# A fused linear-attention and mixture-of-experts kernel on eight cores: another order of the experts, of the queue and of the small inputs

## The chip, the cores and the metric

The kernel runs on all eight cores of one Trainium2 chip. No core talks to another: core c takes one half of batch element c // 2, 1024 tokens that it writes, and reads the other half of that sequence as well, because the attention state sums over it. The metric is the device time of the slowest core in microseconds (us).

## The reference

Layer one is linear attention with 16 query heads over 4 key/value heads of width 128, on hidden states (4, 2048, 2048). In the kernel's staging each core works on the 2048 tokens of one sequence for K and V and on its own 1024 for everything else:

```
sq, sk = elu(q) + 1, elu(k) + 1
kv = sum over s of sk[s] v[s]^T ;  k_sum = sum over s of sk[s]
attn = (sq @ kv) / (sq . k_sum + 1e-6) ;  y = x + attn @ Wo.T ;  x2 = layernorm(y)
```

Layer two is a mixture of experts on x2, closed by a second layer norm:

```
h = x2 @ down_w ;  logits = x2 @ router_w - cost ;  top 2 of 8 experts, gates by softmax
out = sum over 2 picks of gate * (gelu(gelu(h) @ w1_e) @ w2_e + b2_e)      (w1_e: 1024 x HE[e])
out += 0.1 * (gelu(gelu(h) @ shared_w1) @ shared_w2)
y2 = x2 + out @ up_w + gelu(x2) @ core_w ;  result = layernorm(y2)
```

An expert that a token did not pick sees a zero row, and what it makes of a zero row is added too; the kernel takes that from one row of each expert's output (the "zero rows") by a small matmul with coefficients. HE is [1024, 2048, 3072, 4096] twice over, so experts 0 to 7 have 1, 2, 3, 4, 1, 2, 3, 4 groups of 1024 hidden units, 20 groups in all.

## The kernel before

**Weights.** All weights lie in HBM as float32. GpSimd's queue (called POOL in the profile) loads them in quarters of a block: one DMA of 128 x 2048 elements, 1 MB read and cast to 0.5 MB of bfloat16. Two quarters are a half. A group of an expert has four halves, two of w1 and two of w2.

**Stages.** (1) K and V of the four 512-token blocks, in the order 2, 3, 0, 1; block 2 is done quarter by quarter as its data lands, block 3 waits for all its four quarters. (2) Q, (3) the output projection Wo with residual and the sums for the layer norm, for token halves th = 0 and 1. (4) `router(0)` reads the float32 x2 of th 0; `down_tile(th, lc)` computes gelu(h) per 128 columns; `ln_stats` and `ln1_tile` normalize th 1 between them; then `router(1)`, `logits` and `routing`, which gives each token its two slots in the gather area `xg`. `grow_tile(ti)` transposes gelu(h) to token rows, and 16 scatters on POOL (8 tiles of 128 tokens, two picks) write them to `xg`. (5) The shared expert's first matrix, `shared1`, on TensorE. (6) The 20 groups: `xg_load` (on SyncE's queue, SP) and `xg_transpose` bring an expert's rows in; `gemm1` works on C = CAP[e] slots (448, 320, 256, 192, twice), `gemm2` on tiles of up to 128 of them; `y_store` writes `yd`. Between them lie `turn`, 8 calls that transpose x2 for the output, and `core_tile`, 32 tiles of gelu(x2) @ core_w, by the tables TURN and CORE. (7) The tail: `gather_low` and `gather_high` fetch each token's two rows of `yd`; the second shared matrix, the zero rows (`Rr`) and the gathered rows are summed in PSUM (`combine` scales and adds the gathered rows); then 8 tiles of 4 x 8 matmuls with up_w, the layer norm and the stores.

**Order of the weights.** `stream` is the list of halves in order of use: 80 for the experts, 2 for shared_w2 (SW2), 4 for up_w (UP0, UP1). `stream_into(slot, token)` puts the next half into a slot that comes free. Ten halves are placed ahead: C1 twice, B1 twice, D, B0 twice, E twice, S. `used` refills a slot after its last matmul, except the B slots, which become the store of gelu(x2), and D, which then holds core_w. So five half slots (C1, C1, E, E, S) carry the stream through the experts. POOL's queue is served in order: an instruction that waits holds all behind it. The scatters stand behind the two loads into B0, which wait for `t_d1`, the last down tile. `gather_low` stands in the stream, at group 17; `zero_row(e)`, a 2 KB load each, after each expert.

**Small inputs.** Ten small tensors and the matrix `sel` are loaded on SP at the start, 1.2 MB, unordered against the weights and x.

Of the kernel before, what the change touches and what calls it, by code (L numbers as in the profile page):

```python
# [29 lines left out]
BASE = np.cumsum([0] + CAP).tolist()  # L30
MAIN = BASE[NE]
# [3 lines left out]
GROUPS = [(e, g) for e in range(NE) for g in range(HE[e] // 1024)]  # L35
# [77 lines left out]
def build_nc():  # L113
# [9 lines left out]
    bq_t = din("bq_t", (128, 16))  # L123
    bk_b = din("bk_b", (128, 512))
    bv_b = din("bv_b", (128, 512))
    down_b_t = din("down_b_t", (128, 8))
    up_b_t = din("up_b_t", (128, 16))
    core_b_t = din("core_b_t", (128, 16))
    b1_t = din("b1_t", (128, NCH_TOT + 8))
# [44 lines left out]
    bqs = sb("bqs", (128, 16), F32)  # L174
    dbs = sb("dbs", (128, 8), F32)
    ubs = sb("ubs", (128, 16), F32)
    cbs = sb("cbs", (128, 16), F32)
# [1 line left out]
    b1s = sb("b1s", (128, NCH_TOT + 8), F32)
    rbb = sb("rbb", (128, 64), F32)  # L180
    cf = sb("cf", (128, 472), F32)
    ch = sb("ch", (128, 384), BF16)
# [1014 lines left out]
    xg_load(0)  # L1197
    xg_transpose(0)
    xg_load(1)
    for gi, (e, g) in enumerate(GROUPS):  # L1200
# [4 lines left out]
        if last and e + 1 < NE:
            xg_transpose(e + 1)
            if e + 2 < NE:
                xg_load(e + 2)
        for _ in range(CORE.get(gi, (0, 0))[0]):
            core_tile()  # L1210
        gemm2(gi)
        for th, q in TURN.get((gi, 2), []):
            turn(th, q)
        if last:
            y_store(e)
            if e:
                zero_row(e - 1)
        if e == NE - 2 and last:
            t_ylow = list(t_ydma)
# [8 lines left out]
    t_lastmm = u_free  # L1230
# [185 lines left out]

    for over, src in ((True, yd.ap()), (False, yd.ap()[0:MAIN, :])):
        kept = po.branch(None)
        if over:
            gather_low(src)  # L1420
        gather_high(src)
        po.join(kept, flg[0:1, 0:1], over)
# [86 lines left out]
def _stage_weights(inp):  # L1509
# [24 lines left out]
    m["bq_t"] = col(inp["L0_attn_bq"])  # L1534
    m["bk_b"] = f(np.broadcast_to(inp["L0_attn_bk"], (128, 512)))
    m["bv_b"] = f(np.broadcast_to(inp["L0_attn_bv"], (128, 512)))
    m["down_b_t"] = col(g("down_b"))
    m["up_b_t"] = col(g("up_b"))
    m["core_b_t"] = col(g("core_b"))
    m["b1_t"] = f(np.concatenate([col(g(f"e{e}_b1")) for e in range(NE)]  # L1540
                                 + [col(g("shared_b1"))], axis=1))
# [53 lines left out]
```

How the kernel before makes its waits and increments, by code:

```python
    def after(self, *toks):  # L63
        for tok in toks:
            if tok is None:
                continue
            c, val = tok
            if self.seen.get(id(c), 0) >= val:
                continue
            self.seen[id(c)] = val
            self.q.append(lambda eng, h=c.h, val=val: eng.wait_ge(h, val))
# [5 lines left out]
    def step(self, fn, *toks):  # L77
        self.after(*toks)
        c = self.count
        c.v += 1
        self.q.append(lambda eng, h=c.h: fn(eng).then_inc(h, 1))
        return (c, c.v)
# [1 line left out]
    def dma(self, c, out, in_, *toks):  # L84
        self.after(*toks)
        c.v += 16
        self.q.append(lambda eng, h=c.h: eng.dma_start(out, in_).then_inc(h, 16))
        return (c, c.v)
# [877 lines left out]
            def scat(e, ti=ti, k=k):  # L966
                return e.indirect_dma_start(
                    xg.ap(), bass.IndirectOffsetOnAxis(
                        ap=slt[:, k * 8 + ti:k * 8 + ti + 1], axis=0),
                    grow(ti), None).then_inc(c_sc.h, 16)
# [209 lines left out]
    def gather(c, dst, src, i):  # L1180
        return lambda e: e.indirect_dma_start(
            dst, None, src, bass.IndirectOffsetOnAxis(
                ap=slt[:, i:i + 1], axis=0)).then_inc(c.h, 16)
```

## Time and profile before

| | |
|---|---|
| median of 3 runs | 1264.79 us (1262.26 to 1277.39) |
| the profiled execution | 1255.26 us |
| its span, slowest core (core 7) | 1253.7 us |
| spans of the other cores | 1243.4 to 1250.7 us |
| TensorE matmul busy | 1061.4 us (85%) |
| VectorE, ScalarE, GpSimd busy | 432.9, 286.1, 219.2 us |
| POOL's DMA queue | 146.85 MB written, 73.2% of 16 engines' span |
| SP's DMA queue | 38.18 MB written, 9.9% |

The span runs from the first to the last instruction of a core; the time is 1.6 us more. All rows are of core 7. Columns DMA share and GB/s of a stretch say how busy the core's 16 DMA engines were and what they wrote; the share reads 1.07 in long stretches where the queue is never empty, so 1.07 and not 1 stands for full. A cast load counts its 0.5 MB written, not the 1 MB read.

### The profile page before, as it was taken

How to read it: one execution, taken by the hardware profiler on the slowest of the kernel's cores; microseconds unless marked ns; L12 is line 12 of the kernel's file. 1: busy time of each engine (PE TensorE's matmuls, PEld its weight loads, DVE VectorE, ACT ScalarE, POOL GpSimd, SP SyncE). 2: the span in 40 equal slices, each digit the busy share in tenths (PEclk: the TensorE clock that was granted, in tenths of full speed). 3: DMA queues.
4: the chain of work that ended last, by engine and by line, in shares of the span. 5: the costliest groups of instructions: out<-in, count | busy, mean ns of one | idle time of the engine just before them, and what ended most of it. 6: DMA issues, size and time to landing. Idle time of an engine off the chain costs nothing.

```text
span 1253.7 us, 18255 instructions; the slowest of 8 cores (1243.4 to 1253.7 us)
## 1 busy us (share of the span) xinstructions
PE 1061.4 (85%) x7106; PEld 591.7 (47%) x7106; DVE 432.9 (35%) x730; ACT 286.1 (23%) x489; POOL 219.2 (17%) x301
## 2 busy tenths in 40 slices
PE   4699999998999899789989678697987978735897
PEld 1244443433444344345657557563556757412443
DVE  0233334446679673026332111211211211100477
ACT  0100133442223344217221111111111111120234
POOL 7000100000010002401222222211222211511100
PEclk9899999999999999989999999998999988868899
DMA  9999591407269535985999999999999999999235
GB/s 158 168 166 164 83 211 56 68 1 137 65 124 189 100 57 78 235 167 122 192 165 173 180 168 166 180 176 199 165 187 171 162 185 170 204 192 198 94 101 168
DMA packets 95502, 186.29 MB, mean 149 GB/s; under 512 B 8055, under 2 KB 13303, under 8 KB 95408
## 3 DMA queue, kind: packets, MB, share of 16 engines
q0 software_dynamic: 73504, 146.85, 73.2%
q1 hardware_dynamic: 21904, 38.18, 9.9%
q8 instruction: 59, 0.97, 0.3%
q14 instruction: 35, 0.29, 0.1%
HBM read 291.73 MB, written 27.53 MB: 255 GB/s over the span
## 4 chain that ended last, share of the span: by engine, by line
PE 54%; DMA 30%; DVE 7%; issue 4%; POOL 2%; ACT 1%; DVEq 0%; SPq 0%; ACTq 0%; POOLq 0%
PE bk L248 53%; DMA rD<-wts 13%; DMA rC<-wts 7%; DVE ms L263 4%; DMA rE<-wts 3%; DMA rA<-x 3%; DMA smx<-yd 2%; DVE rA L263 2%; PE bk L252 2%; DMA ms<-xg 1%; POOL xg L967 1%; DMA yd<-ms 1%; ACT ms L260 1%; DMA xg<-ms,slt 1%; DVE ms L274 1%
## 5 line engine op out<-in xcount | busy, mean ns | idle before, releaser
L260 ACT ACTIVATE rC<-bk,b1s 128x192 bf16<-128x192 f32 (+3 forms) x160 | 76.7, 480 | 431.6 <-PE bk L248 427.8
L248 PE MATMUL bk<-rC 128*128 128x512 bf16 (+5 forms) x824 | 149.1, 337 | 27.8 <-DMA rC<-wts 26.5
L248 PE MATMUL bk<-rD,rB 128*128 128x128 bf16 x2048 | 126.2, 226 | 33.6 <-DMA rD<-wts 31.6
L248 PEld LDWEIGHTS bk<-rD,rB 128*128 128x128 bf16 x2048 | 122.7, 101 | 39.7 <-issue 38.7
L248 PEld LDWEIGHTS bk<-rC 128*128 128x128 bf16 (+1 forms) x824 | 79.0, 101 | 92.3 <-issue 48.4
L248 PE MATMUL bk<-rE,rC 128*128 128x512 bf16 (+1 forms) x416 | 99.0, 393 | 26.3 <-DMA rE<-wts 25.1
L263 DVE TENSOR_TENSOR rA<-rA,bk 128x512 f32<-128x512 f32 x64 | 43.3, 686 | 190.6 <-PE bk L248 190.6
L87 POOL DMA_DIRECT2D rC<-wts x72 | 51.5, 728 | 253.1 <-PE bk L248 227.8
L248 PE MATMUL bk<-rD,rA 128*128 128x512 bf16 x256 | 63.5, 405 | 29.6 <-DMA rA<-x 22.7
L87 POOL DMA_DIRECT2D rE<-wts x76 | 54.7, 729 | 172.3 <-PE bk L248 166.9
L248 PE MATMUL bk<-rC,rE 128*128 128x192 bf16 (+3 forms) x608 | 78.5, 288 | 1.6 <-DMA rE<-wts 1.6
L248 PEld LDWEIGHTS bk<-rE,rC 128*128 128x128 bf16 (+1 forms) x416 | 41.1, 103 | 80.0 <-issue 38.9
L263 DVE TENSOR_TENSOR ms<-ms,bk 128x512 f32<-128x512 f32 (+1 forms) x52 | 35.6, 685 | 112.1 <-PE bk L248 112.1
L277 DVE COPY ms<-bk 128x512 f32<-128x512 f32 (+2 forms) x50 | 34.5, 689 | 92.3 <-PE bk L248 85.9
L248 PEld LDWEIGHTS bk<-rC,rE 128*128 128x128 bf16 x608 | 55.8, 98 | 21.3 <-issue 2.3
L260 ACT ACTIVATE ms<-ms 128x512 f32<-128x512 f32 (+2 forms) x51 | 30.8, 606 | 123.1 <-DVE ms L267 87.8
L248 PE MATMUL bk<-rA 128*128 128x512 bf16 x256 | 57.9, 379 | 0.0
L248 PE MATMUL bk<-rE,rA 128*128 128x512 bf16 x256 | 57.9, 379 | 0.0
L87 POOL DMA_DIRECT2D rD<-wts x34 | 24.6, 727 | 180.4 <-PE bk L248 165.7
L248 PEld LDWEIGHTS bk<-rD,rA 128*128 128x128 bf16 x256 | 25.6, 103 | 62.3 <-issue 39.1
L248 PE MATMUL bk<-rC,rS 128*128 128x512 bf16 (+2 forms) x352 | 53.2, 309 | 0.0
L87 POOL DMA_DIRECT2D rS<-wts x38 | 27.3, 739 | 134.1 <-PE bk L248 125.1
(128 smaller groups left out, 1262.7 us busy)
## 6 DMA issues: line engine op xcount, KB each, us to landing
rE<-wts POOLq DMA_DIRECT2D x76, 512.0 KB, 27.2
rC<-wts POOLq DMA_DIRECT2D x72, 512.0 KB, 27.1
rS<-wts POOLq DMA_DIRECT2D x38, 512.0 KB, 28.0
rD<-wts POOLq DMA_DIRECT2D x34, 512.0 KB, 25.1
rA<-x POOLq DMA_DIRECT2D x16, 512.0 KB, 49.6
yd<-ms SPq DMA_DIRECT2D x16, 512.0 KB, 9.7
out<-rA SPq DMA_DIRECT2D x32, 256.0 KB, 2.9
rB<-wts POOLq DMA_DIRECT2D x12, 512.0 KB, 12.9
```

What stands on the lines that cost most here:

```text
L87: self.q.append(lambda eng, h=c.h: eng.dma_start(out, in_).then_inc(h, 16))
L248: return lambda e: e.matmul(o, lt, r, start=a, stop=z, skip_group_check=skip)
L252: return lambda e: e.transpose(o, i, idn)
L260: return lambda e: e.activation(o, i, f, **kw)
L263: return lambda e: e.tensor_tensor(o, a, b, op)
L274: return lambda e: e.reciprocal(o, i)
L277: return lambda e: e.tensor_copy(o, i)
L967: return e.indirect_dma_start(xg.ap(), bass.IndirectOffsetOnAxis(ap=slt[:, k * 8 + ti:k * 8 + ti + 1], axis=0), grow(ti), None).then_inc(c ...
```

## The change

1. **Experts.** The order is 3, 2, 1, 0, 4, 5, 6, 7: first 4 groups with C = 192, then 3 with 256, 2 with 320, 1 with 448; the last four experts stay. The slots of `xg` are laid out in that order. TURN and CORE are new tables, `xg_transpose` stands ahead of the turns.
2. **Down tiles.** Tiles 0, 1, 2 of th 0 are computed together, jc by jc (`down3`), each step as soon as its x2 is there; `ln_stats` of th 1 comes after 13 of 16 steps; `router(0)` moves behind down tile 7 and `logits(0)` behind `router(1)`. Router(1) uses bank 3.
3. **Scatters.** Each half of B0 is loaded after four tiles' scatters, not ahead of all 16. The load of b2 ahead of them is gone.
4. **End of the queue.** `gather_low` moves behind the last expert's and SW2's weights. The up weights leave the stream: UP0 is loaded behind the first four `gather_high`, UP1 behind the last four. The zero rows and b2 are loaded by SP after the last matmul of the experts, as float32, and copied to bfloat16 by VectorE.
5. **Small inputs.** Nine tensors become two: the K and V biases (0.5 MB), issued when the second quarter of block 2 has landed, and `sml_t` (0.49 MB), when block 0 has; `sel` follows. Banks of the first K and V tiles are renumbered, so that block 3 starts on banks that are evicted first.

```diff
+ORDER = [3, 2, 1, 0, 4, 5, 6, 7]
+BASE = [sum(CAP[f] for f in ORDER[:ORDER.index(e)]) for e in range(NE)]
-GROUPS = [(e, g) for e in range(NE) for g in range(HE[e] // 1024)]
+GROUPS = [(e, g) for e in ORDER for g in range(HE[e] // 1024)]
...
-        t_ld = sp.dma(c_ld, d_, s_.ap())
+    t_ld = sp.dma(c_ld, msl(0, 1024), bkv.ap(), xb[2][1])
+    t_sm = sp.dma(c_sm, sml[:], sml_t.ap(), xb[0][3])
...
+    KB = [2, 4, 0, 6]
-        kv_evict(s, s, 4 + s, tks[s], tvs[s])
+        kv_evict(s, KB[s], KB[s] + 1, tks[s], tvs[s])
...
+    ac.after(t_sm)
+    dv.after(t_sm)
+    pe.after(t_sm)
...
-    router(0)
-    down_tile(0, 0)
+    def down3(j0, j1):
+        for jc in range(j0, j1):
+            for lc in range(3):
+                pe.after(bfree[lc], dn[0][lc], t_x2b[0][jc])
+                f = mm(bank[lc][:], slot["C0"][:, lc * 2048 + jc * 128:
+                                               lc * 2048 + jc * 128 + 128],
+                       x2b(0, jc), jc == 0, jc == 15)
...
+    down3(0, 13)
     t_stat[1], t_mat = ln_stats(S1[1], S2[1], ys2[1], t_tmp[1])
-    down_tile(0, 1)
-    logits(0)
-    down_tile(0, 2)
+    down3(13, 16)
     for lc in range(3, 8):
         for oc in range(3 * lc - 9, 3 * lc - 6):
             ln1_tile(1, oc)
         t_d0 = down_tile(0, lc)
+    router(0)
     ln1_tile(1, 15)
     t_rtd = router(1)
+    logits(0)
...
-    stream += [(b, h) for b in (SW2, UP0, UP0 + 1) for h in range(2)]
+    stream += [(SW2, 0), (SW2, 1)]
+    spare = []
...
-    stream_into(("B0", 0), t_d1)
-    stream_into(("B0", 1), t_d1)
-    po.dma(c_rr, Rr[8:17, :], b2all.ap(), t_rtd)
...
             po.do(scat)
+        if ti % 4 == 3:
+            stream_into(("B0", ti // 4), t_d1)
...
-    TURN = {(2, 1): [(0, 0)], (2, 2): [(0, 1), (0, 2)], (3, 1): [(0, 3), (1, 0)],
-            (3, 2): [(1, 1), (1, 2)], (4, 1): [(1, 3)]}
-    CORE = {4: (0, 2), 5: (1, 1), 6: (1, 2), 7: (1, 2), 8: (1, 2), 9: (1, 2),
+    TURN = {(2, 1): [(0, 0), (0, 1)], (2, 2): [(0, 2), (0, 3)],
+            (3, 1): [(1, 0), (1, 1)], (3, 2): [(1, 2), (1, 3)]}
+    CORE = {3: (0, 1), 4: (1, 2), 5: (1, 2), 6: (1, 2), 7: (0, 1), 8: (0, 1),
             11: (0, 1), 12: (0, 1), 13: (1, 2), 14: (1, 2), 15: (1, 2),
-            16: (1, 2), 17: (1, 1)}
+            16: (1, 2), 17: (1, 2), 18: (1, 2)}
...
-        if gi == max(CORE):
-            po.after(t_co[0], *t_ylow)
-            gather_low(yd.ap()[0:BASE[NE - 1], :])
+    po.after(t_co[0], *t_ylow)
+    kept = po.branch(None)
+    gather_low(yd.ap()[0:BASE[ORDER[-1]], :])
...
+    R32 = rC[0:17, 0:1024]
+    sp.after(t_lastmm)
+    for e in range(NE):
+        sp.dma(c_rr, R32[e:e + 1, :], yd.ap()[BASE[e]:BASE[e] + 1, :], t_row0[e])
+    t_rr = sp.dma(c_rr, R32[8:17, :], b2all.ap())
-    t_R = [zero_row(NE - 1)]
+    t_R = [dv.step(cp(Rr[0:17, :], R32), t_rr, t_rtd)]
...
+    for th in range(2):
+        for over, src in ((True, yd.ap()), (False, yd.ap()[0:MAIN, :])):
+            kept = po.branch(None)
+            if over and th == 0:
+                gather_low(src)
+            gather_high(src, th)
+            po.join(kept, flg[0:1, 0:1], over)
+        for h in range(2):
+            hs, free = spare[2 * th + h]
+            load_half((UP0 + th, h), hs, *free)
```

## Rows read from the trace of the kernel before

**Rows 1.** The page's slices: busy tenths in 40 slices of the span.
```profile
PE   4699999998999899789989678697987978735897
DMA  9999591407269535985999999999999999999235
```

**Rows 2.** Stretches: length, busy us of each engine, TensorE's granted clock, DMA share, GB/s.
```profile
487.00:495.00 8.00, 6.42 (x54) 3.77 (x53) 2.15 (x10) 2.87 (x4) 3.15 (x5) 1.00 0.09 14
545.00:595.00 50.00, 49.40 (x289) 26.59 (x287) 24.62 (x48) 27.38 (x51) 6.16 (x9) 1.00 0.63 128
595.00:1158.00 563.00, 441.16 (x4138) 314.51 (x4135) 98.42 (x147) 79.55 (x162) 129.15 (x180) 0.93 1.07 179
1180.00:1200.00 20.00, 19.34 (x114) 9.39 (x112) 8.07 (x15) 2.36 (x5) 0.00 (x0) 1.00 0.00 1
```

**Rows 3.** Timeline of PE, the opening: start, us, operation, idle before and its releaser.
```profile
14.93 5.24 PE L248 MATMUL bk<-rD,rA 128*128 128x512 bf16 x16 [14.93 <-DMA rA<-x]
26.85 3.61 PE L248 MATMUL bk<-rD,rA 128*128 128x512 bf16 x16 [3.22 <-DMA rA<-x]
45.53 5.30 PE L248 MATMUL bk<-rD,rA 128*128 128x512 bf16 x16 [2.33 <-DMA rA<-x]
61.21 5.99 PE L248 MATMUL bk<-rD,rA 128*128 128x512 bf16 x16 [6.93 <-DVE rB L271]
```

**Rows 4.** Timeline of PE, router and down tiles, then from shared1 to gemm1 of expert 0.
```profile
413.28 3.59 PE L248 MATMUL bk<-rA,smx 128*32 128x512 f32 x26 [0.31 <-DMA smx<-rw]
424.58 3.63 PE L248 MATMUL bk<-rB,rC 128*128 128x512 bf16 x16
428.05 1.88 PE L248 MATMUL bk<-ms,cf 128*128 128x512 f32 x4
459.78 1.02 PE L248 MATMUL bk<-rA,smx 128*32 128x512 f32 x2 [0.38 <-DVE rA L263]
494.71 27.79 PE L248 MATMUL bk<-rS,rE 128*128 128x512 bf16 x128
539.55 14.41 PE L248 MATMUL bk<-rC 128*128 128x448 bf16 x64 [0.68 <-DVE rC L277]
```

**Rows 5.** Timeline of POOL and DVE: the slots are written, B0's loads, first and last of 16 scatters.
```profile
484.37 0.44 DVE L263 TENSOR_TENSOR slt<-ms 128x8 int32<-128x8 f32 x2
491.85 2.87 POOL L87 DMA_DIRECT2D rB<-wts  x4 [12.56 <-PE bk L252]
495.97 1.06 POOL L967 DMA_INDIRECT xg<-ms,slt  x1 [0.71 <-ACT ms L260]
514.53 0.96 POOL L967 DMA_INDIRECT xg<-ms,slt  x1 [0.27 <-issue]
```

**Rows 6.** One load into a free queue (issued at 548.55): us from issue to landing.
```profile
DMA to landing us min/median/max: 6.4/6.4/6.4
```

**Rows 7.** Timeline of PE: gemm1 at C = 192, gemm1 and gemm2 at C = 448; two core tiles.
```profile
757.53 5.44 PE L248 MATMUL bk<-rC,rE 128*128 128x192 bf16 x64
825.71 12.27 PE L248 MATMUL bk<-rC 128*128 128x448 bf16 x64
839.80 14.33 PE L248 MATMUL bk<-rE,rC 128*128 128x512 bf16 x64
660.39 7.31 PE L248 MATMUL bk<-rD,rB 128*128 128x128 bf16 x128
```

**Rows 8.** Timeline of PE, last group and tail.
```profile
1096.47 1.48 PE L248 MATMUL bk<-rC,rD 128*128 128x192 bf16 x16 [1.24 <-DMA rD<-wts]
1116.16 5.94 PE L248 MATMUL bk<-rE,rC 128*128 128x512 bf16 x16 [18.21 <-DMA rE<-wts]
1122.61 3.73 PE L248 MATMUL bk<-rE,rC 128*128 128x512 bf16 x16 [0.50 <-DMA rE<-wts]
1163.74 3.57 PE L248 MATMUL bk<-rC,smx 17*128 17x512 bf16 x8 [17.00 <-DMA smx<-yd]
1241.60 3.62 PE L248 MATMUL bk<-rE,rC 128*128 128x512 bf16 x16
```

More of the change, by code:

```diff
@@ L29 @@
 CAP = [448, 320, 256, 192, 448, 320, 256, 192]
[L30 to L31 removed]
+ORDER = [3, 2, 1, 0, 4, 5, 6, 7]
+BASE = [sum(CAP[f] for f in ORDER[:ORDER.index(e)]) for e in range(NE)]
+MAIN = sum(CAP)
 OVER = (MAIN + np.cumsum([0] + [1025 - c for c in CAP])).tolist()
 ROWS = OVER[NE]
[L35 removed]
+GROUPS = [(e, g) for e in ORDER for g in range(HE[e] // 1024)]
 NG = len(GROUPS)
+NSML = 952
 WQ0, WO0, DN0, SW1, CO0 = 2, 6, 10, 12, 13
@@ L122, in build_nc @@
     x4 = din("x4", (4, 4, 2, 128, 1024))
[L123 to L129, printed above, removed]
+    bkv = din("bkv", (128, 1024))
+    sml_t = din("sml_t", (128, NSML))
     b2all = din("b2all", (9, L))
     rw32 = din("rw32", (128, 512))
-    rb_b = din("rb_b", (128, 64))
-    cst_f = din("cst_f", (128, 472))
-    cst_h = din("cst_h", (128, 384), BF16)
     sel_h = din("sel_h", (48, 2048), BF16)
@@ L172, in build_nc, with part @@
     cin = {k: [cnt(f"c{k}_{q}") for q in range(4)] for k in slot}
[L174 to L177, printed above, removed]
+    sml = sb("sml", (128, NSML), F32)
     bsum = sb("bsum", (128, 16), F32)
[L179 to L182, printed above, removed]
+    def part(a, n):
+        return sml[:, a:a + n]
+    bqs, dbs, ubs, cbs = part(0, 16), part(16, 8), part(24, 16), part(40, 16)
+    b1s = part(56, NCH_TOT + 8)
+    rbb, cf = part(224, 64), part(288, 472)
+    ch = part(760, 192).bitcast(BF16)
     epsc = sb("epsc", (128, 1), F32)
@@ L362, in build_nc @@
     tks, tvs = [None] * 4, [None] * 4
+    KB = [2, 4, 0, 6]
     for q in range(4):
-        for wsl, wt, b0, tt_ in ((wkc, wk, 0, tks), (wvc, wv, 4, tvs)):
+        for wsl, wt, b0, tt_ in ((wkc, wk, 0, tks), (wvc, wv, 1, tvs)):
             pe.after(wt[q], xb[2][q])
@@ L367, in build_nc @@
                 for jc in range(4 * q, 4 * q + 4):
-                    f = mm(bank[b0 + s][:], xs(2, jc, s), wsl(jc),
+                    f = mm(bank[KB[s] + b0][:], xs(2, jc, s), wsl(jc),
                            jc == 0, jc == 15)
@@ L635, in router @@
     def router(th):
-        pe.after(bfree[5], t_rw)
+        pe.after(bfree[5 - 2 * th], t_rw)
         for jc in range(16):
             q = jc % 4
-            f = mm(bank[5][32 * q:32 * q + 32, :], rws[:, jc * 32:(jc + 1) * 32],
+            f = mm(bank[5 - 2 * th][32 * q:32 * q + 32, :], rws[:, jc * 32:(jc + 1) * 32],
                    y1(th, jc), jc < 4, jc >= 12)
@@ L642, in router @@
             tr = pe.step(f)
-        t_lg[th] = dv.step(cp(lgt[th], bank[5][:]), tr)
-        bfree[5] = t_lg[th]
+        t_lg[th] = dv.step(cp(lgt[th], bank[5 - 2 * th][:]), tr)
+        bfree[5 - 2 * th] = t_lg[th]
         return tr
@@ L700, in grow_tile @@
         bfree[bi] = t_gr[ti]
-    router(0)
-    down_tile(0, 0)
+    def down3(j0, j1):
[5 more added lines that the diff above has]
+                       x2b(0, jc), jc == 0, jc == 15)
+                if jc == 15:
+                    td = pe.step(f)
+                    t_gT[0][lc] = ac.step(act(gT(0, lc), bank[lc][:], AF.Gelu,
+                                              bias=dbs[:, lc:lc + 1]), td,
+                                          wo_done[1][2])
+                    bfree[lc] = t_gT[0][lc]
+                else:
+                    pe.do(f)
+    down3(0, 13)
     t_stat[1], t_mat = ln_stats(S1[1], S2[1], ys2[1], t_tmp[1])
-    down_tile(0, 1)
-    logits(0)
-    down_tile(0, 2)
+    down3(13, 16)
+    nd = 3
     for lc in range(3, 8):
@@ L762, in routing @@
         nonlocal t_r
-        d1(tt(lg, bank[4][:, 0:64], rbb[:], ALU.add), t_lgm[7], t_tmp[0], t_tmp[1])
+        d1(tt(lg, bank[4][:, 0:64], rbb, ALU.add), t_lgm[7], t_tmp[0], t_tmp[1])
         bfree[4] = t_r
@@ L900, in stream_into @@
             npos += 1
+        else:
+            spare.append((hs, free))
     have_co = {}
@@ L912, in build_nc @@
     t_yb = [[None] * 16, [None] * 16]
-    t_bs = dv.step(tt(bsum[:], ubs[:], cbs[:], ALU.add))
+    t_bs = dv.step(tt(bsum[:], ubs, cbs, ALU.add))
     t_idf = dv.step(cp(idf, idb), t_mat)
@@ L1187, in gather_low @@
             po.do(gather(c_gl, glo(ti), src, ti))
-    TURN = {(2, 1): [(0, 0)], (2, 2): [(0, 1), (0, 2)], (3, 1): [(0, 3), (1, 0)],
-            (3, 2): [(1, 1), (1, 2)], (4, 1): [(1, 3)]}
-    CORE = {4: (0, 2), 5: (1, 1), 6: (1, 2), 7: (1, 2), 8: (1, 2), 9: (1, 2),
+    TURN = {(2, 1): [(0, 0), (0, 1)], (2, 2): [(0, 2), (0, 3)],
+            (3, 1): [(1, 0), (1, 1)], (3, 2): [(1, 2), (1, 3)]}
+    CORE = {3: (0, 1), 4: (1, 2), 5: (1, 2), 6: (1, 2), 7: (0, 1), 8: (0, 1),
             11: (0, 1), 12: (0, 1), 13: (1, 2), 14: (1, 2), 15: (1, 2),
-            16: (1, 2), 17: (1, 1)}
-    xg_load(0)
-    xg_transpose(0)
-    xg_load(1)
+            16: (1, 2), 17: (1, 2), 18: (1, 2)}
+    xg_load(ORDER[0])
+    xg_transpose(ORDER[0])
+    xg_load(ORDER[1])
     for gi, (e, g) in enumerate(GROUPS):
         last = g == HE[e] // 1024 - 1
+        p = ORDER.index(e)
         gemm1(gi)
+        if last and p + 1 < NE:
+            xg_transpose(ORDER[p + 1])
+            if p + 2 < NE:
+                xg_load(ORDER[p + 2])
         for th, q in TURN.get((gi, 1), []):
             turn(th, q)
[L1205 to L1208, printed above, removed]
         for _ in range(CORE.get(gi, (0, 0))[0]):
@@ L1215, in build_nc @@
             y_store(e)
[L1216 to L1219, printed above, removed]
+            if p == NE - 2:
+                t_ylow = list(t_ydma)
         for _ in range(CORE.get(gi, (0, 0))[1]):
             core_tile()
-        if gi == max(CORE):
-            po.after(t_co[0], *t_ylow)
-            kept = po.branch(None)
-            gather_low(yd.ap()[0:BASE[NE - 1], :])
-            po.join(kept, flg[0:1, 0:1], False)
+    po.after(t_co[0], *t_ylow)
+    kept = po.branch(None)
+    gather_low(yd.ap()[0:BASE[ORDER[-1]], :])
+    po.join(kept, flg[0:1, 0:1], False)
     t_lastmm = u_free
     t_yall = list(t_ydma)
-    assert nco == 32 and npos == len(stream), (nco, npos, len(stream))
+    assert nco == 32 and npos == len(stream) and len(spare) == 4
     fPE, fAC, fDV = cnt("fPE"), cnt("fAC"), cnt("fDV")
@@ L1364, in combine, with gather_high @@
                             accb_free[b])
-    def gather_high(src):
-        for ti in range(8):
-            if ti >= 4:
+    def gather_high(src, th):
+        for ti in range(4 * th, 4 * th + 4):
+            if th:
                 po.after(t_acc[ti - 4])
@@ L1414, in build_nc @@
     t_sh2 = t
[L1417 to L1422, printed above, removed]
+    for th in range(2):
[8 more added lines that the diff above has]
+            load_half((UP0 + th, h), hs, *free)
     def stat(ti, a, n):
@@ L1533, in _stage_weights @@
     col = lambda a: f(a.reshape(-1, 128).T)
[L1534 to L1541, printed above, removed]
+    parts = [col(inp["L0_attn_bq"]), col(g("down_b")), col(g("up_b")),
+             col(g("core_b"))]
+    parts += [col(g(f"e{e}_b1")) for e in range(NE)] + [col(g("shared_b1"))]
+    m["bkv"] = f(np.broadcast_to(np.concatenate([inp["L0_attn_bk"],
+                                                 inp["L0_attn_bv"]]), (128, 1024)))
     m["b2all"] = f(np.stack([g(f"e{e}_b2") for e in range(NE)] + [g("shared_b2")]))
@@ L1545, in _stage_weights @@
     m["rw32"] = rw.reshape(128, 512)
-    m["rb_b"] = f(np.broadcast_to(np.tile(g("router_b"), 8), (128, 64)))
+    parts.append(np.broadcast_to(np.tile(g("router_b"), 8), (128, 64)))
     cost = np.array([2 * 1024 * h for h in HE], np.float32) * np.float32(1e-7)
@@ L1554, in _stage_weights @@
     cf[:, 200:264] = np.tile(-cost, 8)
-    base, cap, over = np.array(BASE[:8]), np.array(CAP), np.array(OVER[:8])
+    base, cap, over = np.array(BASE), np.array(CAP), np.array(OVER[:8])
     cf[:, 264:336] = np.tile(base + 1.0, 9)
@@ L1564, in _stage_weights @@
     h[:, 256:384] = 1.0
-    m["cst_h"] = h.astype(ml_dtypes.bfloat16)
+    parts += [cf, h.astype(ml_dtypes.bfloat16).view(np.float32)]
+    m["sml_t"] = f(np.concatenate(parts, axis=1).astype(np.float32))
     s = np.zeros((48, 16, 128), np.float32)
```

8 lines of the change are left out of this document (1 added, 7 removed).

## The prediction

> **What bounds the kernel now.** I read the slices first [rows 1]. TensorE is nearly full up to slice 16 and again in the last slices; from slice 19 to slice 37 the DMA engines are full and TensorE is not. Then the stretches [rows 2]: from 595 to 1158 us the DMA share is 1.07, its full value, while TensorE is busy 441 of 563 us. So for 563 us the in-order stream of weights is the bound, and what an engine does there counts only if it keeps the stream from running. In the 50 us ahead of it the share is 0.63: the slots for weights are full, TensorE is busy 49.4 us on expert 0 with C = 448, and the stream stands. Its 8 us at 487 to 495 are emptier still (0.09). Behind 1180 the engines move nothing while TensorE works 19.34 of 20 us. The kernel is bound in turn by TensorE (to 545), by the stream, and by TensorE (from 1170). A stretch in which one of them idles ahead of its turn as the bound is what a new order can win.
>
> **A quarter's price.** In the opening, five quarters lie between the waits that end at 45.53 and 61.21 [rows 3]: 15.68 / 5 = 3.14 us each. All below goes by it.
>
> **1. Small inputs.** TensorE waits for block 3's last quarter until 61.21; the row's releaser is a VectorE step, but that bank's eviction was over at 61.0 and block 3's matmuls need all four quarters, whose spacing fits. The first x quarter is second in the queue. Into a free queue a load lands 6.4 us after issue [rows 6]; with the first issue at 1.6, quarter two would be there at 1.6 + 6.4 + 3.1 = 11.1, and it came at 14.93 less the 0.1 of the start: 3.7 late. The next three took 11.92 (14.93 to 26.85) and not 9.4: 2.5 more. So 1.2 MB of small inputs cost 6.2 us. The K and V biases remain ahead of block 3, 0.5 of 1.2 MB, 2.6 us; `sml_t` and `sel` come when TensorE has block 3 to work on for 29 us. Gain **3.6**; ends 0 (the early lateness is start-up of the queue) and 6.2. TensorE is then busy without a break that depends on DMA until the router, so it arrives there. The renumbered banks gain nothing: block 3's data, not its banks, come last.
> The Trainium skill (DMA: Bandwidth & Descriptors, "Anatomy of one DMA") fits a DMA as 2.0 us plus bytes over 436 GB/s; an estimate by that gives 0.68 MB fewer bytes a price of 1.6 us, and the sum below would be 48.9. No run here shows a small input's price alone yet.
>
> **2. Down tiles.** Router(0) needs the last x2 of th 0, and holds TensorE from 413.28 to 424.58, 11.3 us for 5.6 us of work (router(1) takes that when it need not wait). Now 39 matmuls of three tiles run there at 3.63 / 16 = 0.22 us each, to 421.6; the sums for the statistics are ready at 420.5, so the statistics' matmuls start 6.5 us earlier than their 428.05 [rows 4]. VectorE's chain of 16 normalizations hangs on them and ends router(1) at 460.8; TensorE has only 89 matmuls (19.3) and router(0) (5.6) to do beside it, 448 against 454.3, so the chain still sets the end. `logits(0)` then follows, 0.9. Gain **5.6**; ends 3 and 6.5. Routing and slots come as much earlier.
>
> **3. Scatters, the first experts and the stream's idle time.** The slots are written at 484.8, yet the first scatter goes at 495.97, behind B0's four loads that wait for the last down tile (491.85); the last goes at 514.53 and lands 8.5 later, and rows of `xg` then take their way on SP while three halves compete. TensorE, done with shared1 at 522.5, starts gemm1 at 539.55 [rows 4, 5]: 17 us. In the new order scatters 1 to 8 go from 487 to 497, two B0 quarters, scatters 9 to 16 to 508; landed by about 513, `xg` rows (two tiles, not four) by 522. gemm1 can start at 525 in the old coordinates. SP and POOL both lose the b2 and zero-row loads, 2 to 18 KB each: nothing.
> This would be worth nothing if the stream were already running; it is not. Its idle time is 8 x (1 - 0.09/1.07) = 7.3 and 50 x (1 - 0.63/1.07) = 20.6, together 28 us [rows 2]. With expert 3 first, a group costs TensorE 5.44 + 7.2 = 12.6 us (gemm2 has 32 matmuls, half of the 14.33 row) against 26.6 for expert 0 [rows 7], so the first free slots come 2.7 and 5.4 us after gemm1's start, at 528 and 531 and not at 548.6 and 554.6, while the halves for E and S, issued at 523, still run to 542. Followed half by half: two C1 halves to 554, two core quarters (issued 541) to 561, then E, E, S issued at 551 to 557 and so on; the eight turns make groups 2 and 3 cost TensorE 25 and 28 us, as much as their 25 us of weights, with 15 us of backlog kept. I leave 3 us of idle time for the first eight scatters (1.2 us apart, 0.8 us of transfer each) and 2 for the gap ahead of E. Gain **23**; ends 8 (only the scatters' part) and 28. Experts 1, 0, 4, 5 in sequence are six groups, 151 us of TensorE with their core tiles, against 150 of weights, 6 of core_w and some 30 of stored and gathered rows: the stream stays the bound.
>
> **4. gather_low behind the last weights.** It reads 4 MB between group 19's last w1 quarter (1096.47) and its first w2 half (1116.16): 19.7 - 2 x 3.14 = 13.4 us in which the last expert waits [rows 8]. Removed from there, T0, the landing of the last expert weights (1122.6 now), comes **13.4** earlier; ends 10 and 14. TensorE keeps up: behind gemm2 of group 18 two core tiles (7.3, [rows 7]) end as gemm1's data are there. The work comes back in the tail.
>
> **5. The tail, from T0.** Now: TensorE waits 17.00 us for the last zero row, a 2 KB load behind all of POOL's backlog, and ends at 1245.2, T0 + 122.6 [rows 8]. New, by the queue: SW2 12.6, gather_low 13.4, four gather_high 6.7, UP0 12.6, four gather_high 6.7, UP1 12.6, stores of `yd` 2.5: the last up weights land at T0 + 67.1. TensorE by then has passed: th 0's sum at T0 + 38, th 1's at T0 + 58, tile 0's first three quarters; it still has 8 matmuls and seven tiles at 4 x 1.73 = 6.9, so 1.7 + 48.4, and ends at T0 + 117.2. Gain **5.4**; ends -3 (a wait behind which the clock is half, as in the 5.94 us for 16 matmuls after the 18.21 us wait where 3.7 is usual, and a slower gather) and 10. The SP loads of the zero rows wait for the last store, some 15 us behind T0, and are hidden under gather_low, as is VectorE's copy of 17 x 1024. The four branches on POOL cost issue time only.
>
> **Sum.** 3.6 + 5.6 + 23 + 13.4 + 5.4 = 51.0 us off the profiled 1255.3, which stands 9.5 us under the median; off the median, 1264.8 - 51.0 = **1213.8**.
>
> **The rivals.**
> A. *The idle time is not won.* The stream is given its weights early, yet TensorE in groups 2, 3 and in 9, 10 (twice C = 448, with `yd` stores of four buffers each behind one another) falls behind and the slots fill again. For it: the turns are packed in two groups, and the backlog there is small. Against it: 595 to 1158 shows TensorE busy at 78%, and 35 us of spare time in groups 7 to 12. It gives 3.6 + 5.6 + 13.4 + 5.4 and at most 8 of part 3: 1264.8 - 36 = 1229; with part 1 at 0 and the tail at -3 as well, 1241. Chance 0.15 for 1226 to 1239, 0.12 for about 1241 to 1260.
> B. *The tail grows.* UP1 is last of an in-order queue and TensorE waits for it; if gathers into busy memory take twice 13.4 for each 4 MB, the tail is T0 + 144, and of part 4 nothing is left in the end: 1264.8 - 32 + 8 = 1241. Counted in A's second share.
> C. *Slower.* Core tiles: now 16 loads of core_w into two quarters of D, each tile waiting in TensorE's order with the groups' slots held behind it. If with short groups each of the 16 lets the queue run dry, every one costs the 6.4 us of a load into a free queue less the 3.14 of a running one and the wait ahead, up to 6.4. From 51.0 / 16 = 3.2 us each the change is a loss; at 6.4 it is 1264.8 - 51 + 102 = 1316. Against it: the same loads now run three tiles to a group with the share at 1.07. Chance 0.04 for over 2% slower.
> D. *It does not do what it says*: the scatters still end late, since their slots or rows, not B0's loads, hold them. The rows contradict that (484.8 against 495.97).
>
> **How the numbers follow.** The forecast, with its own range of 1202 to 1226 from the ends of the five parts taken together, has 0.69; A's near part 0.15; A's far part and B 0.12; C 0.04. The 8-in-10 range reaches into A: 1200 to 1238. About 2% is what a measurement of this kernel tells from no change; below 1239.5 is faster by that: 0.84; within 0.12; slower 0.04.
>
> **What would show it.** Block 3's matmuls start near 57.5 and not 61.2; router(1) ends near 451 (9 us less); the gap from shared1 to gemm1 falls from 17 to about 3 us; no stretch of 50 us with a share under 0.9 between gemm1's start and T0; T0 near 1077 of the span; nothing of gather_low ahead of it; the last up weights 67 us behind T0 and TensorE's end 117 behind it; a span of about 1203. Wrong would be: a share that sags in groups 2, 3, 9 or 10 (A), a tail over T0 + 125 (B), waits for rD<-wts with a share below 1 (C).

## The result and the profile after

| | before | after |
|---|---|---|
| median | 1264.82 us | 1223.28 us |
| ratio | | 0.9673, 95% interval 0.9607 to 0.9738 |
| profiled execution | 1255.26 us | 1222.89 us |
| its span, slowest core | 1253.7 us (core 7) | 1221.3 us (core 2) |

The forecast was 1213.8 us in a range of 1200 to 1238. The direction and the range held; of the 51.0 us forecast, 41.5 came in the medians, and 32.4 between the two profiled executions, in which the terms can be followed. The slowest core is another one than before, so the steps below are means over the cores. Medians and ratios here are of fast executions; in a slower state some cores show a lower granted clock and take longer, and two cores that did so in the profiled execution of e2 (0 and 1) and of e5 (6 and 7), at 0.93, are left out of the means.

The page's slices of the changed kernel, busy tenths in 40 slices, against [rows 1]:
```profile
PE   5599999998999899988898698976977877876897
...
DMA  9999593406249816899999999999999999999934
```
Counted from 1, the DMA engines are full from slice 18 on, where before they were full from slice 20 to 37. TensorE's weak slices 36 and 37 (3 and 5) now read 7 and 6.

Stretches of core 2: length, busy us of PE, PEld, DVE, ACT, POOL, granted clock, DMA share, GB/s. Against [rows 2]:
```profile
487.00:500.00 13.00, 11.42 (x77) 6.02 (x76) 3.12 (x12) 4.87 (x7) 9.92 (x11) 1.00 0.46 165
...
545.00:595.00 50.00, 43.40 (x361) 32.23 (x359) 27.82 (x52) 29.04 (x64) 11.57 (x16) 1.00 1.07 166
595.00:1095.00 500.00, 413.78 (x3904) 293.64 (x3902) 91.31 (x136) 65.45 (x132) 106.06 (x147) 0.95 1.06 176
```
The share of 0.63 at 545 to 595 has become 1.07. The 13 us up to 500 are still half empty (0.46).

Timeline of core 2's PE, the router's stretch and the step to the experts, against [rows 4]: start, us, operation, idle before and releaser.
```profile
397.80 13.98 PE L245 MATMUL bk<-rC,rB 128*128 128x512 bf16 x64
413.98 0.38 PE L245 MATMUL bk<-rB,rC 128*128 128x512 bf16 x1 [2.20 <-ACT rB L257]
417.38 9.76 PE L245 MATMUL bk<-rB,rC 128*128 128x512 bf16 x38 [3.03 <-DVE rA L260]
426.98 1.88 PE L245 MATMUL bk<-ms,sml 128*128 128x512 f32 x4
428.69 2.11 PE L245 MATMUL bk<-rB,rC 128*128 128x512 bf16 x9
433.52 5.30 PE L245 MATMUL bk<-rB,rC 128*128 128x512 bf16 x16 [2.72 <-ACT rS L257]
...
494.49 27.79 PE L245 MATMUL bk<-rS,rE 128*128 128x512 bf16 x128
526.43 1.01 PE L249 MATMUL bk<-sml,ms 128*128 128x128 bf16 x8 [4.15 <-DMA ms<-xg]
...
529.61 7.01 PE L245 MATMUL bk<-rC 128*128 128x192 bf16 x64 [0.68 <-DVE rC L274]
```
The three tiles do not start at the end of Wo (411.8) but at 413.98 with one matmul and with the others at 417.38, behind a VectorE step, and the next tile waits once more (433.52), for ScalarE's gelu. From shared1's end (522.3) to gemm1 there are now 7.3 us and not 17.0. The 16 scatters are issued from 487.65 to 508.41, as forecast, so rival D (they stay late) is out.

The tail of core 2, against [rows 8]:
```profile
1094.57 3.73 PE L245 MATMUL bk<-rS,rC 128*128 128x512 bf16 x16 [1.42 <-DMA rS<-wts]
1102.34 0.62 PE L249 MATMUL bk<-sml,wc 128*32 128x128 bf16 x8 [4.04 <-issue]
...
1118.49 1.90 PE L245 MATMUL bk<-rC,smx 17*128 17x512 bf16 x8
1127.84 1.01 PE L245 MATMUL bk<-sml,ms 128*128 128x128 bf16 x8 [7.46 <-DVE ms L268]
...
1160.91 3.57 PE L245 MATMUL bk<-rS,rC 128*128 128x512 bf16 x8 [3.39 <-DMA rS<-wts]
...
1210.94 1.89 PE L245 MATMUL bk<-rS,rC 128*128 128x512 bf16 x8
```
The last expert weights are there at 1094.6. The zero rows (1118.49) cost no wait any more; the gathered rows cost 7.46 us, the last up weights 3.39, and the 8 matmuls after that wait take 3.57 us where later ones take 1.89. The last up weights come 66.3 us behind the last expert weights, and TensorE ends 118.3 us behind those (67.1 and 117.2 forecast). The last expert weights themselves were forecast for 1077 and came at 1094.6.

**The steps in numbers.** Each is the mean over the cores of one profiled execution: the start of block 3, of the statistics' matmuls (stat.), of shared1, of the first gemm1; the end of the last expert matmul; the DMA engines' idle time from 480 us to that end (over stretches of 2 us with a share under 0.95, the length times 1 - share/1.07); the end of TensorE.

| kernel | block 3 | stat. | shared1 | gemm1 | experts' end | DMA idle | PE's end |
|---|---|---|---|---|---|---|---|
| before | 61.5 | 429.0 | 495.7 | 538.4 | 1120.7 | 30.0 | 1239.5 |
| after | 58.9 | 427.0 | 495.0 | 528.9 | 1098.4 | 12.7 | 1209.9 |
| e1_order_only | 61.3 | 428.7 | 495.4 | 534.6 | 1105.9 | 15.2 | 1224.5 |
| before (cores 2 to 7) | 61.6 | 429.2 | 495.9 | 538.6 | 1121.7 | 30.7 | 1240.7 |
| e2_gather_low_only (cores 2 to 7) | 61.2 | 428.7 | 495.4 | 538.0 | 1108.3 | 28.9 | 1240.8 |
| e5_tail_only (cores 0 to 5) | 62.8 | 431.3 | 498.0 | 540.2 | 1116.7 | 32.5 | 1229.9 |
| e6_scatters_back | 60.3 | 428.4 | 495.8 | 534.4 | 1106.2 | 15.9 | 1217.3 |
| e7_router_back | 60.0 | 427.5 | 495.8 | 531.3 | 1103.9 | 13.5 | 1216.7 |
| e8_after | 59.6 | 427.5 | 495.5 | 529.5 | 1102.8 | 12.0 | 1215.5 |
| e9_three_banks | 60.1 | 420.6 | 490.8 | 524.3 | 1100.6 | 12.4 | 1211.8 |
| e10_small_first | 61.5 | 429.9 | 497.6 | 534.8 | 1110.3 | 16.3 | 1221.0 |
| e11_best | 59.9 | 420.7 | 491.0 | 524.8 | 1097.0 | 12.3 | 1205.1 |
| e12_after_again | 59.8 | 428.0 | 496.0 | 531.8 | 1105.7 | 13.9 | 1217.3 |

The runs were made in three sets: e1 to e4 (before: 1260.6 us), e5 to e8 (1268.8) and e9 to e12 (1269.5), the last on another chip than the first two. The changed kernel's own steps differ by up to 7.3 us between the sets (experts' end), so a step is compared inside its set where that is possible. The second and third set have no profile of the kernel before.

**shared1 is held up on one die.** In every one of these executions the 128 matmuls of shared1 take 27.8 to 28.0 us on the cores of one die, and on at least three cores of the other die 29.2 to 44.2 us. Core 7 of the changed kernel, start, us, operation, idle before and releaser:
```profile
509.87 3.42 PE L245 MATMUL bk<-rS,rE 128*128 128x512 bf16 x8 [3.63 <-ACT rD L257]
515.14 20.88 PE L245 MATMUL bk<-rS,rE 128*128 128x512 bf16 x96 [1.86 <-ACT rD L257]
...
537.75 5.44 PE L245 MATMUL bk<-rC 128*128 128x192 bf16 x64 [0.94 <-DVE rC L274]
```
TensorE waits for ScalarE, which itself has stood idle for 5.61 us before its eviction at 509.04; what it waits for, no trace or run shows. In the kernel before this cost nothing that can be seen: gemm1 starts at 537.8 us in the mean of cores 0 to 3, which have it, and at 538.9 in that of cores 4 to 7, which do not and wait for the rows of `xg`. In the changed kernel shared1's end sets gemm1 on the cores that have it (532.2, 525.4 and 537.8 on cores 5 to 7; 523.3 to 529.6 on cores 0 to 4), and cores 5 and 7 end the experts at 1106.1 and 1106.8, against 1097.0 in the mean of cores 0 to 4. So a mean over eight cores holds some of this, and where it matters the undisturbed cores are given beside it.

### The profile page after: what moved, and what is told of

Read it like the earlier page. It is cut to its first block, busy times and chain, and to the rows that moved or that the text cites. A ratio compares the mean times of both kernels' runs of the same rounds, so it can differ in the third digit from the quotient of the medians.

```text
span 1221.3 us, 18253 instructions; the slowest of 8 cores (1208.3 to 1221.3 us)
## 1 busy us (share of the span) xinstructions
PE 1054.5 (86%) x7106; PEld 592.1 (48%) x7106; DVE 434.4 (36%) x731; ACT 281.5 (23%) x487; POOL 214.7 (18%) x292
## 4 chain that ended last, share of the span: by engine, by line
PE 51%; DMA 35%; DVE 5%; issue 4%; POOL 3%; ACT 1%; DVEq 0%; POOLq 0%; ACTq 0%; SPq 0%
PE bk L245 50%; DMA rC<-wts 11%; DMA rD<-wts 10%; DMA rS<-wts 7%; DMA rA<-x 4%; DVE ms L260 3%; PE bk L249 2%; DMA ms<-yd,slt 1%; DVE rA L260 1%; POOL xg L984 1%; DMA ms<-xg 1%; DMA xg<-ms,slt 1%; DMA yd<-ms 1%; DVE rA L274 0%; POOL rA L90 0%
## 5 line engine op out<-in xcount | busy, mean ns | idle before, releaser
L257 ACT ACTIVATE rC<-bk,sml 128x192 bf16<-128x192 f32 (+3 forms) x160 | 76.8, 481 | 434.8 <-PE bk L245 430.9
L245 PE MATMUL bk<-rE,rC 128*128 128x512 bf16 (+1 forms) x408 | 92.2, 379 | 6.3 <-DMA rE<-wts 6.3
L245 PE MATMUL bk<-rC,rE 128*128 128x192 bf16 (+4 forms) x640 | 86.6, 294 | 2.0 <-DMA rE<-wts 2.0
L245 PEld LDWEIGHTS bk<-rC,rE 128*128 128x128 bf16 x640 | 58.8, 98 | 26.5 <-issue 2.9
L245 PE MATMUL bk<-rS,rC 128*128 128x512 bf16 (+1 forms) x248 | 59.0, 390 | 11.1 <-DMA rS<-wts 9.8
L245 PE MATMUL bk<-rC,rS 128*128 128x512 bf16 (+3 forms) x352 | 54.2, 311 | 0.0
(121 smaller groups left out, 1211.8 us busy)
## 6 DMA issues: line engine op xcount, KB each, us to landing
rC<-wts POOLq DMA_DIRECT2D x72, 512.0 KB, 27.8
rB<-wts POOLq DMA_DIRECT2D x12, 512.0 KB, 12.4
```

The lines of the kernel that those rows point to most:

```text
L245: return lambda e: e.matmul(o, lt, r, start=a, stop=z, skip_group_check=skip)
L257: return lambda e: e.activation(o, i, f, **kw)
```

## The experiments

**e1, the experts' order alone.** The table of core tiles ends by group 17, so that gather_low stays where it was.
```diff
-GROUPS = [(e, g) for e in range(NE) for g in range(HE[e] // 1024)]
+GROUPS = [(e, g) for e in ORDER for g in range(HE[e] // 1024)]
...
+    CORE = {3: (0, 1), 4: (1, 2), 5: (1, 2), 6: (1, 2), 7: (1, 2), 8: (0, 2),
+            11: (0, 1), 12: (0, 1), 13: (1, 2), 14: (1, 2), 15: (1, 2),
+            16: (1, 2), 17: (1, 2)}
```


> The kernel before with the new order of the experts, the turns in groups 2 and 3 and all core tiles by group 17, nothing else of the change. Theory (the stream's idle time): short groups free the slots sooner, so the idle time of the DMA engines between 500 and 600 us, 20 us before (mean of three cores), falls under 8 us, gemm1 starts about 2 us sooner (two tiles to transpose and not four), and the kernel takes 12 us less (8 to 16). Rival (turns packed into two groups make TensorE the bound, the slots fill again): idle time over 12 us and the time within 4 us of before.


Ratio 0.9863 (0.9772 to 0.9953), 17 us less, a little over the 8 to 16 expected. Stretches of its slowest core, columns as above:
```profile
500.00:545.00 45.00, 35.62 (x206) 19.84 (x204) 2.10 (x4) 13.29 (x23) 19.70 (x23) 0.89 1.00 218
545.00:595.00 50.00, 44.86 (x367) 32.45 (x365) 28.70 (x54) 29.58 (x66) 11.57 (x16) 1.00 1.07 168
```
TensorE is busy 45 of 50 us and the share is 1.07: the slots did not fill again, and the rival is out. The idle time fell by 14.8 us and the experts' end by 14.8 (on cores whose shared1 ran through, the idle time fell from 30.5 to 12.2). gemm1 came 3.8 us sooner.

**e2, gather_low alone.**
```diff
-        if gi == max(CORE):
+        if gi == NG - 2:
```


> The kernel before with gather_low alone moved, from group 17 to behind group 18, so that it stands behind the last expert's weights and SW2; the up weights stay ahead of gather_high. Theory (the end is a sum of one queue): the last expert weights land 13 us sooner, but gather_high stands behind gather_low and both up blocks, so the first sum over experts waits for it, and the end of TensorE is unchanged: time 0 (-3 to +3). Rival (each part is worth its own term): 13 us less.


Ratio 1.0010 (0.9955 to 1.0064). On cores 2 to 7 the experts' end moves 13.4 us ahead, and the tail behind it grows by 13.5, from 119.0 to 132.5. Timeline of PE, core 2:
```profile
1106.64 3.73 PE L248 MATMUL bk<-rE,rC 128*128 128x512 bf16 x16 [0.92 <-DMA rE<-wts]
...
1161.41 3.57 PE L248 MATMUL bk<-rC,smx 17*128 17x512 bf16 x8 [30.52 <-DMA smx<-yd]
1164.92 3.59 PE L248 MATMUL bk<-ch,ms 128*128 128x128 bf16 x32
```
What came sooner waits 30.52 us for a zero row, a 2 KB load behind the gathers and the up weights; the four gathered tiles are there by then (3.59 us for their 32 matmuls, without a wait). Moving the load without the rest of part 4 wins nothing, as expected.

**e3 and e4, the stream by itself.** Both leave out the computation and write zeros to the output, beside which GpSimd loads 96 quarters. In e3 all cores load, in e4 only the even ones.
```diff
+    for n in range(96):
+        t_q[n % 16] = po.dma(cq[n % 16], two(q[n % 16]),
+                             wsrc(17 + n // 4, n % 4), t_q[n % 16])
+    po.join(kept, flg[0:1, 0:1])
-        im["on"] = np.array([[1]], np.int32)
+        im["on"] = np.array([[1 - c % 2]], np.int32)
```


> Only the stream: GpSimd's queue loads 96 quarters of the expert weights on every core, 16 in flight, and the output is written with zeros; all the rest of the computation is left out. Theory (the two cores that share a memory stack bound the stream): 3.1 us a quarter. Rival (the core's own DMA engines bound it): 3.1 as well; the next run tells them apart.

> As the run before, but only the even cores load; the odd ones only write zeros. Theory (shared memory): a quarter takes 2.6 us or less on the even cores. Rival (own engines, for a cast load): 3.1 us as with all cores.


Core 0 of e3 (length, busy us of DVE and POOL, granted clock, DMA share, GB/s):
```profile
150.00:200.00 50.00, 0.00 (x0) 10.84 (x16) 1.00 1.08 168
```
Core 0 of e4:
```profile
100.00:150.00 50.00, 0.00 (x0) 12.86 (x18) 1.00 1.12 209
...
250.00:300.00 50.00, 0.00 (x0) 7.14 (x10) 1.00 0.67 105
```
A quarter writes 0.524 MB: 3.12 us at 168 GB/s with all cores loading, 2.51 at 209 with only the even ones. So with all cores loading a quarter's price is set by something that cores share and not by a core's own engines, although the share reads as full in both. That it is the pair of cores, and not the die or the chip, no run separates: e4 stops every odd core. The Trainium skill (HBM Reference, Specifications (TRN2)) says that a core streaming alone gets about 425 GB/s and each of a pair about 358. Reads are twice the written bytes here, 336 and 418 GB/s, and the runs agree. The 209 holds only for the first 150 to 250 us: then three of the four even cores slow down (to 0.67 and 105 on core 0), at different times, and end at 348 to 395 us, later than any core of e3 (341 to 343). No run shows why, and each was run once.

**e5, the whole tail alone** (part 4 of the change on the kernel before).
```diff
-    stream += [(b, h) for b in (SW2, UP0, UP0 + 1) for h in range(2)]
+    stream += [(SW2, 0), (SW2, 1)]
...
+            load_half((UP0 + th, h), hs, *free)
```


> The kernel before with the whole of part 4 and nothing else: gather_low behind the last weights, UP0 and UP1 behind the gathers, zero rows by SyncE. Theory: last expert weights 13 us sooner and a tail shorter by 5 (TensorE ends 114 to 117 us behind them and not 119): 18 us less (15 to 21). Rival (the up weights behind the gathers hold TensorE in the first tiles, so the tail grows by what it is relieved of): 8 us less or nothing.


Ratio 0.9853 (0.9833 to 0.9874), 18.7 us less, and TensorE's tail is 1229.9 - 1116.7 = 113.2 us and not 118.8: both about as expected, and the rival is out. That the experts end 13 us sooner is not shown by this run: against the profile before, of another set, they end 4.0 sooner, and this execution was 2.3 late at shared1 already.

**e6, B0's loads ahead of the scatters again.**
```diff
-        if ti % 4 == 3:
-            stream_into(("B0", ti // 4), t_d1)
+    stream_into(("B0", 0), t_d1)
+    stream_into(("B0", 1), t_d1)
```


> The changed kernel with B0's two loads put ahead of all 16 scatters again. Theory (the earlier scatters let the stream and gemm1 start sooner): gemm1 starts 6 us later and the time is 5 us more (3 to 8) than the changed kernel's. Rival (the stream is the bound and the same bytes are only reordered): under 2 us more.


Ratio 0.9796 (0.9763 to 0.9829) against 0.9733 of e8 beside it: 6.9 us more by the medians (1240.6 and 1233.7). The scatters' place is worth something even with the experts' order in place. Where it is won is less clear. In the mean gemm1 starts 4.9 us later, the idle time is 3.9 more and the experts' end 3.4 later. On cores 0 to 3, whose shared1 ran through in both, gemm1 starts 6.1 later (532.7 and 526.6), but the idle time is only 1.3 more (12.2 and 10.9) and the experts end at the same time (1100.7 and 1100.9).

**e7, the router's old order.**
```diff
-    down3(0, 13)
+    router(0)
+    down_tile(0, 0)
     t_stat[1], t_mat = ln_stats(S1[1], S2[1], ys2[1], t_tmp[1])
```


> The changed kernel with the router, the first three down tiles and logits(0) in the order of before. Theory (the three tiles together wait for the last bank that VectorE evicts and for ScalarE's gelu, so part 2 of the change costs and does not gain): shared1 starts 2 us sooner and the time is 1 to 2 us less than the changed kernel's. Rival (part 2 gains as predicted and the loss is elsewhere): 5 us more.


Ratio 0.9701 (0.9681 to 0.9720), e8's is 0.9733 (0.9712 to 0.9753). The intervals overlap, and the steps are those of e8 within 0.4 us up to shared1, which did not come 2 us sooner as expected. Part 2 as it was made is worth nothing; whether it costs a little is open.

**e8 and e12, the changed kernel again**, as the measure of each set.


> The changed kernel itself, as the measure for the two runs beside it: 0.967 of before.

> The changed kernel itself, as the measure for the three runs beside it: 0.967 to 0.973 of before.


Ratios 0.9733 (0.9712 to 0.9753), where 0.967 was expected, and 0.9705 (0.9689 to 0.9720), inside what was expected.

**e9, three other banks for the three tiles.**
```diff
-                pe.after(bfree[lc], dn[0][lc], t_x2b[0][jc])
-                f = mm(bank[lc][:], slot["C0"]
+                pe.after(bfree[3 + lc], dn[0][lc], t_x2b[0][jc])
+                f = mm(bank[3 + lc][:], slot["C0"]
```


> The changed kernel with the three down tiles in banks 3, 4, 5, which are free since the attention heads, instead of 0, 1, 2, which the last Wo tiles hold until VectorE evicts them. Theory (part 2 of the change failed on its banks): the tiles start at the end of Wo, the statistics' matmuls 4 to 5 us sooner against the end of Wo, no wait for gelu behind them, shared1 5 us sooner, and the time 3 to 5 us under the changed kernel's. Rival (VectorE's backlog of normalizations sets the stage whatever TensorE does): shared1 within 1 us and the time the same.


Ratio 0.9653 (0.9625 to 0.9682), e12's 0.9705. Timeline of PE, core 0:
```profile
402.67 9.88 PE L245 MATMUL bk<-rC,rB 128*128 128x512 bf16 x45
412.39 8.58 PE L245 MATMUL bk<-rB,rC 128*128 128x512 bf16 x39
420.80 1.88 PE L245 MATMUL bk<-ms,sml 128*128 128x512 f32 x4
422.52 5.56 PE L245 MATMUL bk<-rB,rC 128*128 128x512 bf16 x25
```
39 matmuls in 8.58 us from the end of Wo on, the statistics at 420.8: these are the prediction's own numbers for part 2. shared1 starts 5.2 us sooner than in e12, the experts end 5.1 sooner, and the median is 5.2 less (1226.7 and 1231.8).

**e10, the small inputs at once.**
```diff
-    t_ld = sp.dma(c_ld, msl(0, 1024), bkv.ap(), xb[2][1])
-    t_sm = sp.dma(c_sm, sml[:], sml_t.ap(), xb[0][3])
+    t_ld = sp.dma(c_ld, msl(0, 1024), bkv.ap())
+    t_sm = sp.dma(c_sm, sml[:], sml_t.ap())
```


> The changed kernel with its two tensors of small inputs and sel loaded at once at the start, without the waits for x. Theory (1.2 MB ahead of block 3 cost the opening what its bytes cost): block 3 starts 2.5 us later and the time is 2 to 3 us more than the changed kernel's. Rival (it is the many short rows of the ten old tensors that cost, not their bytes): block 3 within 1 us of the changed kernel's.


Block 3 starts 1.7 us later than in e12 (61.5 and 59.8; e9 and e11, with the same opening as e12, have 60.1 and 59.9), and the ratio is 0.9714 (0.9697 to 0.9732) against 0.9705: in the step it shows, in the time it does not. The rival, under 1 us, is out; the theory's 2.5 was too much.

**e11, three banks and the up tiles in another order**, the version that the experiments point to.
```diff
+    for ti, oq in [(0, 0), (0, 1), (1, 0), (1, 1), (2, 0), (2, 1),
+                   (0, 2), (0, 3)]:
+        up_mm(ti, oq)
```


> The three banks, and the up matmuls of tiles 0, 1, 2 that use UP0 ahead of all that use UP1. Theory (TensorE waits 3.4 us for UP1 in tile 0, then runs 8 matmuls at half its clock): the wait goes, TensorE's tail is 4 to 5 us shorter than the run with the three banks alone, and the time as much. Rival (VectorE, with its sums, is the bound of the tail): 0 to 2 us.


Ratio 0.9619 (0.9602 to 0.9637), clear of e12's 0.9689 to 0.9720; e9's interval (0.9625 to 0.9682) it just touches. Timeline of PE, core 0, where the tile's third and fourth quarter used to wait for UP1:
```profile
1151.59 1.89 PE L245 MATMUL bk<-rC 128*128 128x512 bf16 x8
1153.32 3.62 PE L245 MATMUL bk<-rE,rC 128*128 128x512 bf16 x16
1156.77 1.89 PE L245 MATMUL bk<-rS,rC 128*128 128x512 bf16 x8
```
No wait and no slow matmuls. The tail is 1205.1 - 1097.0 = 108.1 us, in e9 111.2, in e12 111.6, so 3.1 shorter than e9's where 4 to 5 were expected (4.1 on cores 4 to 7, whose shared1 ran through in both). It beats both kernels: 1220.7 us against 1231.8 for the changed kernel and 1269.5 for the one before, on one chip.

## Why the prediction was right, and where it was not

The median fell inside the range, and what was forecast to be won is won in the places that were named. But the forecast of 1213.8 is nearer to the measurement than its steps are. The experts' end was to move by 3.6 + 5.6 + 23 + 13.4 = 45.6 us and moved by 22.3; with the tail, TensorE's end was to move by 51.0 and moved by 29.6. The medians fell by 9 us more than the profiled executions, because the profiled one of before lay 9.5 us under its median and the one after did not. That was not in the forecast, and that it covers part of what is lacking is luck. By its steps:

1. **Small inputs: 2.6 of 3.6.** That block 3 waits for x, and not for the VectorE step that its row names, is borne out: on core 2 of the changed kernel the row of block 3's start, at 59.58, has 9.87 us idle <-DMA rA<-x. The lateness was attributed in full to the 1.2 MB. e10 has 1.7 us for `sml_t` and `sel`, the same 0.68 MB, loaded at once. The lower number, 1.6, that came from the Trainium skill's fit (DMA: Bandwidth & Descriptors, Anatomy of one DMA) is nearer to e10 than 3.6; the sum by it is 49.0 and not 48.9. That fit is for loads that GpSimd issues, and these are issued by SyncE. What else the 2.6 holds is not shown; executions with the same opening differ by up to 1.4 us. By shared1 only 0.7 of it is left.
2. **Down tiles: nothing of 5.6.** The step that failed is "39 matmuls of three tiles run there ... to 421.6". That needed three free banks at the end of Wo. VectorE was behind by then, and evicted the last Wo tile at 416.45 to 417.13; an interleaved loop needs all its banks at its first step, where `router(0)` had needed none of them. From the end of Wo to shared1 it is 83.8 us now and was 82.0 (495.0 - 411.2 and 495.7 - 413.7). Router(1) ends at 459.7 on core 2, where 451 was forecast. e9 takes away the bank and nothing else, and the forecast comes true: statistics 7.4 us sooner, shared1 5.2.
3. **Idle time of the stream: right in kind, 17.3 us fewer.** Forecast were 23, and 9.2 more from starting sooner, of which 0.7 came. On cores whose shared1 ran through it is 19.0 (from 30.5 to 11.5), and nearly all of that is the order alone: 12.2 are left in e1. What is lacking lies in two places. The engines are still half idle at 487 to 500, where eight scatters go 1.27 us apart. And gemm1 starts 5.3 us behind shared1 in the mean of cores 0 to 4, where 3 was forecast; on core 2 it waits 4.15 and 0.92 us for its first rows. On the other die shared1 itself ends late, at up to 536.0 us against 522.0 in the mean of cores 0 to 4, which was not in the forecast.
4. **gather_low behind the weights: 13.4 of 13.4 by itself, about 5 in the whole change.** Alone (e2) it moved the experts' end by 13.4. In the whole change the experts' end moved by 22.3, of which 17.3 is idle time and 5.0 is left. The busy time from 480 us on is 1098.4 - 480 - 12.7 = 605.7 us after and 610.7 before, for 109 and 113 MB written; e2 needed 1108.3 - 480 - 28.9 = 599.4. The 6.3 us between e2 and the changed kernel are not located: the rate of the busy stream, 179.8 GB/s, is 178.4 in e12 for the same kernel on another chip, so such a difference can hide as much.
5. **Tail: 4.6 of 5.4 where the experts end undisturbed, 7.3 in the mean.** Queue by queue it is as forecast (last up weights at 66.3 of 67.1 us on core 2). On cores 0 to 4 the tail is 114.3 us and was 118.9; cores 5 and 7, which came late to the experts' end, have 106.8 and 103.5 and make the mean look better than the forecast. That moving the gathers pays only with the up weights behind them was in the sum and is shown by e2 and e5.

The parts are not quite additive: by the medians the order alone (e1) gives 17 us and part 4 alone (e5) 18, together 35, and the whole change in the set of e5 gives 35.1, although e6 puts 6.9 on the scatters' place.

Rival A (slots fill again) is out by e1, and C (core tiles let the stream run dry) by the share of 1.06 over 500 us. B would have been right for gather_low moved alone in what it says of the end, a tail that grows by as much as the weights gain; that the gathers would be slow did not come true (66.3 us to the last up weights where 67.1 were forecast).

## What to carry to other kernels

Look for the engine that idles just ahead of the stretch in which it is the bound, and feed it there: here an order of the same work gave 1.4% (0.5 to 2.3). A move out of an in-order queue is worth its time only if nothing that the end waits for then stands behind it. Before tiles are interleaved, ask when the last of their accumulators comes free, and who frees it.

## What the runs showed that was not expected

- A full DMA share does not say what bounds a stream: 3.12 us a quarter with all cores loading and 2.51 with only the even ones, at shares of 1.08 and 1.12 (e3, e4).
- shared1 is 1 to 16 us longer on most cores of one die than on the other. Such a delay is hidden as long as the next stage waits for something else anyway. Once the change had taken that wait away, it decided when gemm1 starts on those cores.
- A wait can cost more than its length, where TensorE's granted clock is half behind it. On core 2 of the changed kernel it is 0.50 (1.2 GHz) in the 3.4 us after the wait for the last up weights: 3.57 us for 8 matmuls, 1.89 otherwise, so 1.7 us on top of 3.39 of waiting. Ahead of the wait, and again from 1164.5 on, it is 1.00. In e11, without the wait, there is neither.
